# Slot attention with all six products of kept attention and decays on VectorE, and new orders of the four engines' lists

## The reference

```python
q = short_conv(h @ Wq, cq); k = short_conv(h @ Wk, ck)      # 4 taps, silu
v = short_conv(h @ Wv, cv); w = l2norm(short_conv(h @ Ww, cv))
g = log_sigmoid(h @ Wf1 @ Wf2); beta = sigmoid(h @ Wb)
# per head, over the 64 positions of a sequence:
Sk = Sk * exp(g)[None, :] + k[:, None] * (beta * w)[None, :]   # keys by slot
Sv = Sv * exp(g)[:, None] + (beta * w)[:, None] * v[None, :]   # values by slot
a  = softmax(q @ Sk * SCALE)                                   # over the slots
o  = a @ Sv
out = (o * rsqrt(mean(o * o) + eps) * norm_w * sigmoid(gate)) @ Wo
```

## Time and profile before

| | us |
|---|---|
| median of 3 runs | 6353.45 |
| the profiled execution | 6398.69 |
| its span | 6396.9 |
| slot attention in it | from about 80 to 4050 |
| one head of it (four pairs) | 246.8 |
| mean granted TensorE clock of the span | 0.964 |

### The profile page before, as it was taken

The page is one execution under the profiler, slowest core; times in us unless marked ns, Lnnn a source line. Parts: engine busy times, 40 slices in busy tenths (PEclk is TensorE's granted clock), DMA queues, the critical chain, the costliest instruction groups (busy, mean ns, idle before and its releaser), DMA issues. The chain is left out here.

```text
span 6396.9 us, 126892 instructions
## 1 busy us (share of the span) xinstructions
PE 5836.3 (91%) x45072; PEld 4550.3 (71%) x45072; DVE 4333.3 (68%) x8987; ACT 3753.7 (59%) x8473; POOL 1931.1 (30%) x2390
## 2 busy tenths in 40 slices
PE   8999999999999999999999999786889989988879
PEld 5777777777777777777777777675665666667546
DVE  5777777777777777777777777566762237766513
ACT  5677766767766776766777666453651434444313
POOL 2333333333333333333333333232113310001233
PEclk9999999999999999999999999887999999999989
DMA  6200000000000000000000000000002255010124
GB/s 209 65 2 6 5 2 6 4 3 6 1 6 7 1 6 6 2 6 6 2 6 5 2 6 1 28 15 28 2 2 78 91 162 172 2 32 15 60 72 154
DMA packets 164245, 205.77 MB, mean 32 GB/s; under 512 B 22891, under 2 KB 149612, under 8 KB 162928
## 3 DMA queue, kind: packets, MB, share of 16 engines
q1 hardware_dynamic: 148592, 159.99, 8.1%
q0 software_dynamic: 12960, 34.63, 1.5%
q10 hardware_dynamic: 2016, 2.37, 0.1%
HBM read 158.14 MB, written 114.16 MB: 43 GB/s over the span
## 5 line engine op out<-in xcount | busy, mean ns | idle before, releaser
L1713 POOL TENSOR_TENSOR gsa_amb<-gsa_aab,gsa_yb 128x256 f32<-128x256 f32 x64 | 59.9, 937 | 867.7 <-ACT gsa_aab L1565 867.7
L1735 POOL TENSOR_TENSOR gsa_ama<-gsa_aaa,gsa_ya 128x256 f32<-128x256 f32 x64 | 62.4, 975 | 803.0 <-ACT gsa_aaa L1634 803.0
L1548 ACT ACTIVATE gsa_gwva<-PSA,gsa_wcv 128x1024 f32<-128x1024 f32 x64 | 71.2, 1113 | 374.9 <-PE PSA L967 374.9
L1624 ACT ACTIVATE gsa_gwvb<-PSA,gsa_wcv 128x1024 f32<-128x1024 f32 x64 | 71.2, 1113 | 295.8 <-PE PSA L1123 295.8
L955 PE MATMUL PSA<-XT,gsa_wa 128*128 128x512 f32 x256 | 150.0, 716 | 46.7 <-issue 38.5
L1719 POOL TENSOR_TENSOR gsa_ssa<-gsa_ssa,gsa_neghalf 128x4 f32<-128x4 f32 x64 | 64.7, 1011 | 304.3 <-DVE gsa_ssa L1350 304.3
L455 ACT ACTIVATE ffn0b_sl<-PSA 128x512 f32<-128x512 f32 x48 | 28.7, 597 | 207.0 <-PE PSA L162 207.0
L1740 POOL TENSOR_TENSOR gsa_ssb<-gsa_ssb,gsa_neghalf 128x4 f32<-128x4 f32 x64 | 64.4, 1007 | 269.2 <-DVE gsa_ssb L1475 269.2
L263 DVE TENSOR_TENSOR ffn0b_hidden<-ffn0b_sl,PSA 128x512 f32<-128x512 f32 x48 | 33.0, 687 | 163.8 <-ACT ffn0b_sl L455 163.8
L2181 POOL TENSOR_TENSOR mlstm_rs<-mlstm_wide,mlstm_neghalf 128x16 f32<-128x16 f32 x32 | 95.3, 2980 | 140.9 <-DVE mlstm_wide L2058 140.9
L1928 PE MATMUL PSA<-mlstm_XC,mlstm_WIF 128*128 128x128 f32 x512 | 95.5, 363 | 45.7 <-ACT mlstm_XC L2093 45.7
(11 more groups left out here) (758 smaller groups left out, 20366.6 us busy)
## 6 DMA issues: line engine op xcount, KB each, us to landing
pairs<-in_blank SPq DMA_DIRECT2D x2, 35904.0 KB, 126.4
ffn0b_XS<-pairs SPq DMA_DIRECT2D x71, 132.0 KB
ffn1b_XS<-pairs SPq DMA_DIRECT2D x71, 132.0 KB
gsa_wa<-in_w_heads SPq DMA_DIRECT2D x16, 512.0 KB, 3.6
X<-in_x SPq DMA_DIRECT2D x8, 512.0 KB, 6.8
mlstm_CX<-in_ctx SPq DMA_DIRECT2D x32, 128.0 KB, 2.1
ffn0b_WGU<-results SPq DMA_DIRECT2D x8, 512.0 KB, 5.3
ffn0b_WD<-results SPq DMA_DIRECT2D x8, 512.0 KB, 6.0
```

## The change

Only lists in `gsa` change; no shape, buffer, or DMA does.

1. The three products of kept attention and decays that GpSimd did (levels 2, 8 and 32, `AM[:, 0]`, `AM[:, 2]`, `AM[:, 4]`) are issued by VectorE. The semaphores `reach_a_by_pool` and `reach_b_by_pool` go; `reach_a_by_dve` counts six.
2. VectorE's list, from the end of the first three convolution steps on: products 0 and odd, a convolution, product 1, the remaining convolutions (the three of the queries now follow each other), product 4, the identity's, product 2, the first masked copy, decay 0, the norm's sum, product 3, masked copy 2, decay 1, masked copies 3, 4, 5 and 6, decays 2 and 3. Decay 4 goes ahead of the first level addition, and the level step of blocks of 8 ahead of the residual addition.
3. TensorE's list: the two first projections trade places around the last slots product; the two gate products trade places; the transposes of the values and the product of keys and queries stand right behind the transposes of the slot keys; the transposes of decay 1 go ahead of the readout; the first slots product goes ahead of the sum of squares. The waits on GpSimd's masks are for the sixth and the seventh at the first two decayed slots products.
4. ScalarE's list: the two sigmoids trade places; the silu of keys and queries goes ahead of the squares and the first decay's copy; the scaled product of keys and queries ahead of decay 2's copy; the readout's square and the copy of decay 4 behind decay 3's.
5. GpSimd's list: without the three products; the masks in the order odd, diagonal, 3, 2, 4, 0, 1.

The core of the diff, for the half in which slice b is projected and slice a finished (the other half has the same edits):

```diff
 # TensorE
+                        pe.wait_ge(reach_a_by_dve, n * 6 + 3)
+                            last = nc.tensor.matmul(PS[1][:, j * 64:(j + 1) * 64], tile(Ya[:, 1, 512:1024], j), AMa[:, 1, ...
-                        pe.wait_ge(reach_a_by_pool, n * 3 + 2)
                             last = nc.tensor.matmul(PS[0][:, j * 64:(j + 1) * 64], tile(Ya[:, 0, 512:1024], j), AMa[:, 0, ...
                         pe.wait_ge(silu_b_by_act, n * 2 + 1)
                             last = nc.tensor.transpose(tile(PS[4], j), tile(GWVb[:, 512:1024], j), IDENT[:, :])
+                        pe.wait_ge(conv_b_by_dve, n * 9 + 6)
+                            last = nc.tensor.transpose(tile(PS[7], j), tile(GWVb[:, 1024:1536], j), IDENT[:, :])
+                        pe.wait_ge(silu_b_by_act, n * 2 + 2)
+                            last = nc.tensor.matmul(tile(PS[6], j), tile(QKb[:, 512:1024], j), tile(QKb[:, 0:512], j), ...
+                        pe.wait_ge(reach_a_by_dve, n * 6 + 5)
                         pe.wait_ge(weights_a_by_dve, n * 7 + 2)
                             last = nc.tensor.matmul(PS[2][:, j * 64:(j + 1) * 64], tile(Ya[:, 2, 512:1024], j), AMa[:, 2, ...
...
                             last = nc.tensor.transpose(tile(PS[4], j), tile(Yb[:, 1, 512:1024], j), IDENT[:, :])
+                        pe.wait_ge(weights_a_by_dve, n * 7 + 7)
+                            last = nc.tensor.matmul(tile(PS[1], j), tile(GWVa[:, 1024:1536], j), tile(QKa[:, 512:1024], j), ...
...
-                        pe.wait_ge(masked_b_by_pool, n * 7 + 4)
+                        pe.wait_ge(masked_b_by_pool, n * 7 + 6)
                             last = nc.tensor.matmul(PS[6][:, j * 64:(j + 1) * 64], tile(LTb[:, 1, :], j), AMb[:, 0, ...
+                        pe.wait_ge(masked_b_by_pool, n * 7 + 7)
 # VectorE
+                        nc.vector.tensor_tensor(blocks(AMa[:, 0, :], 2), righttiles(AAa[:, :, 0:128], 2), rightblocks(Ya[:, 0, 0:512], 2), ALU.mult).then_inc(reach_a_by_dve, 1)
...
+                        nc.vector.tensor_tensor(blocks(AMa[:, 4, :], 32), ...
+                        nc.vector.tensor_tensor(blocks(AMa[:, 2, :], 8), ...
                         nc.vector.copy_predicated(halves_odd(QKa[:, 512:1024]), ...
+                        nc.vector.tensor_tensor(spread(Yb[:, 0, :], 1), ...
+                        nc.vector.tensor_scalar(ssb[:, :], ssb[:, :], 1e-6, None, ALU.add).then_inc(wnorm_b_by_dve, 1)
+                        nc.vector.tensor_tensor(blocks(AMa[:, 3, :], 16), ...
                         nc.vector.copy_predicated(right(QKa[:, 512:1024], 2), ...
+                        nc.vector.tensor_tensor(spread(Yb[:, 1, :], 2), ...
                         nc.vector.copy_predicated(right(QKa[:, 512:1024], 4), ...
                         nc.vector.copy_predicated(right(QKa[:, 512:1024], 8), ...
-                        nc.vector.tensor_tensor(spread(Yb[:, 1, :], 2), ...
                         nc.vector.copy_predicated(right(QKa[:, 512:1024], 16), ...
+                        nc.vector.tensor_scalar(den2a[:, :], den2a[:, :], 1e-5, None, ALU.mult).then_inc(onorm_a_by_dve, 1)
                         nc.vector.copy_predicated(right(QKa[:, 512:1024], 32), ...
 # GpSimd
-                        nc.gpsimd.tensor_tensor(blocks(AMa[:, 2, :], 8), ...
-                        nc.gpsimd.tensor_tensor(blocks(AMa[:, 0, :], 2), ...
-                        nc.gpsimd.tensor_tensor(blocks(AMa[:, 4, :], 32), ...
```

More of the change, by code:

```diff
@@ L1004, in pair @@
                         last.then_inc(weights_b_by_pe, 1)
-                        pe.wait_ge(reach_b_by_pool, m * 3 + 2)
+                        pe.wait_ge(reach_b_by_dve, m * 6 + 3)
+                        for j in range(4):
+                            last = nc.tensor.matmul(PS[5][:, j * 64:(j + 1) * 64], tile(Yb[:, 1, 512:1024], j), AMb[:, 1, j * 64:(j + 1) * 64], start=True, stop=True)
+                        last.then_inc(weights_b_by_pe, 1)
                         for j in range(4):
@@ L1018, in pair @@
                         last.then_inc(turned_a_by_pe, 1)
+                        pe.wait_ge(conv_a_by_dve, n * 9 + 6)
+                        for j in range(4):
+                            last = nc.tensor.transpose(tile(PS[3], j), tile(GWVa[:, 1024:1536], j), IDENT[:, :])
+                        last.then_inc(turned_a_by_pe, 1)
+                        pe.wait_ge(silu_a_by_act, n * 2 + 2)
+                        for j in range(4):
+                            last = nc.tensor.matmul(tile(PS[2], j), tile(QKa[:, 512:1024], j), tile(QKa[:, 0:512], j), start=True, stop=True)
+                        last.then_inc(keyquery_a_by_pe, 1)
                     if before:
+                        pe.wait_ge(reach_b_by_dve, m * 6 + 5)
                         pe.wait_ge(weights_b_by_dve, m * 7 + 2)
@@ L1063, in pair @@
                         last.then_inc(turned_a_by_pe, 1)
-                    if before:
-                        pe.wait_ge(onorm_b_by_act, m * 1 + 1)
-                        for j in range(4):
-                            last = nc.tensor.matmul(PS[4][:, j:j + 1], tile(QKb[:, 0:512], j), ones[:, 0:1], start=True, stop=True)
-                        last.then_inc(read_b_by_pe, 1)
-                    if within:
                         pe.wait_ge(masked_a_by_pool, n * 7 + 2)
@@ L1075, in pair @@
                     if before:
+                        pe.wait_ge(onorm_b_by_act, m * 1 + 1)
+                        for j in range(4):
+                            last = nc.tensor.matmul(PS[4][:, j:j + 1], tile(QKb[:, 0:512], j), ones[:, 0:1], start=True, stop=True)
+                        last.then_inc(read_b_by_pe, 1)
                         pe.wait_ge(onorm_b_by_dve, m * 3 + 2)
@@ L1147, in pair @@
                         last.then_inc(weights_a_by_pe, 1)
-                        pe.wait_ge(reach_a_by_pool, n * 3 + 2)
+                        pe.wait_ge(reach_a_by_dve, n * 6 + 3)
+                        for j in range(4):
+                            last = nc.tensor.matmul(PS[1][:, j * 64:(j + 1) * 64], tile(Ya[:, 1, 512:1024], j), AMa[:, 1, j * 64:(j + 1) * 64], start=True, stop=True)
+                        last.then_inc(weights_a_by_pe, 1)
                         for j in range(4):
@@ L1151, in pair @@
                         last.then_inc(weights_a_by_pe, 1)
-                        pe.wait_ge(reach_a_by_dve, n * 3 + 3)
-                        for j in range(4):
-                            last = nc.tensor.matmul(PS[1][:, j * 64:(j + 1) * 64], tile(Ya[:, 1, 512:1024], j), AMa[:, 1, j * 64:(j + 1) * 64], start=True, stop=True)
-                        last.then_inc(weights_a_by_pe, 1)
-                        pe.wait_ge(sigmoid_b_by_act, n * 2 + 1)
+                        pe.wait_ge(sigmoid_b_by_act, n * 2 + 2)
                         pe.wait_ge(silu_b_by_act, n * 2 + 1)
@@ L1195, in pair @@
                         last.then_inc(turned_b_by_pe, 1)
+                        pe.wait_ge(weights_a_by_dve, n * 7 + 7)
+                        for j in range(4):
+                            last = nc.tensor.matmul(tile(PS[1], j), tile(GWVa[:, 1024:1536], j), tile(QKa[:, 512:1024], j), start=True, stop=True)
+                        last.then_inc(read_a_by_pe, 1)
                         pe.wait_ge(decay_b_by_act, n * 5 + 3)
@@ L1201, in pair @@
                         last.then_inc(turned_b_by_pe, 1)
-                        pe.wait_ge(onorm_a_by_act, n * 1 + 1)
-                        for j in range(4):
-                            last = nc.tensor.matmul(PS[0][:, j:j + 1], tile(QKa[:, 0:512], j), ones[:, 0:1], start=True, stop=True)
-                        last.then_inc(read_a_by_pe, 1)
                         pe.wait_ge(masked_b_by_pool, n * 7 + 2)
@@ L1210, in pair @@
                         last.then_inc(slots_b_by_pe, 1)
+                        pe.wait_ge(onorm_a_by_act, n * 1 + 1)
+                        for j in range(4):
+                            last = nc.tensor.matmul(PS[0][:, j:j + 1], tile(QKa[:, 0:512], j), ones[:, 0:1], start=True, stop=True)
+                        last.then_inc(read_a_by_pe, 1)
                         if gp == 0:
```

363 lines of the change are left out of this document (156 added, 207 removed).

## The result

The changed kernel takes 6620.65 us (median of 4 runs, 6615.44 to 6623.99), the kernel before 6355.26 (4 runs): ratio 1.0417, 95% interval 1.0399 to 1.0435. The forecast was 6425 us with 6345 to 6492 as its range: right in sign, wrong in size, 265 us instead of 72. The profiled execution took 6623.99 us with a span of 6621.9.

A forecast was written before the change was run, and what follows sets the result against it. It took TensorE's in-order list to bound slot attention, stalling for ScalarE and VectorE. 0.52 + 0.08 = 0.60 us per half, times 128 = 77 us, less 5, scaled to +71.5 on 6353.45: 6425 us, range 6345 to 6492.

The forecast's parts named there:

- ScalarE's stretch up to the keys' transposes: Softmax transpose to slot keys' transposes, 10.78 us set by gapless ScalarE: change 0, ends -0.1 to +0.2 us.
- The rival on this place: ScalarE's stretch gets shorter through the sigmoids' exchange: at most 0.2 us per half, 6330 us; chance 0.10.
- The prediction's own sign of being wrong: Softmax transpose to slot keys' transposes: a move of more than 0.1 us would show the forecast wrong.
- The readout: Slot keys' transposes to readout: VectorE's last masked copy comes later, so the readout starts 0.52 us late per half.
- 1.03 of VectorE's 1.40 us: VectorE's list before the last masked copy: 1.40 us longer, 1.03 of it for the three products from GpSimd.
- Behind the readout: Readout to first decayed slots product: +0.08 us, 0.05 for VectorE and GpSimd taking turns, 0.03 for the next step.
- The cover of 0.4 us: Behind the readout: ScalarE's scaled keys and queries end about 1108.1, TensorE needs them at 1108.51, covered by 0.4.
- The rival on SBUF's shared side: GpSimd's masks giving way to VectorE delay the seventh mask, square and slots copy: 0.5 us per half, 6489 us; chance 0.14.
- From the product to the next softmax transpose: First decayed slots product (L1220) to the next half's softmax transpose (L972): change 0.
- The sum: Whole half: 0.52 + 0.08 = 0.60 us, times 128 halves = 77 us.

The follow-up runs named there:

- e1: Changed kernel with the two gate products and the two sigmoids back in the old order; 1.0255 of the kernel before.
- e2: Kernel before with one unused semaphore increment on ScalarE between the wait for the first gate product and the first sigmoid; 1.0521.
- e8: Changed kernel with gate products and sigmoids in the old order and GpSimd's seven masks cut to one column (masking left out); 1.0091 of the kernel before.
- e4: Changed kernel with the denominators' factor moved back ahead of masked copy 2; 1.0396 of the kernel before.
- e10: e8 with VectorE's three added products (decays 0, 2 and 4) also cut to four columns; 1.0074 of the kernel before.
- e5: Changed kernel with GpSimd's seven masks cut to one column each (masking left out); 1.0305 of the kernel before.
- e3: Kernel before with only the three products moved from GpSimd to VectorE, all other lists as before; 1.0415.
- e6: e2 with the kept product ahead of the slot keys' transposes computed twice, filling TensorE's stall; 1.0128 of the kernel before.
- e9: Changed kernel with e1's and e4's edits and decay product 2 between masked copies 4 and 5; 1.0175 of the kernel before.

## Why the prediction was wrong

**ScalarE's stretch up to the keys' transposes: the step that failed.** The prediction took 0 (-0.1 to +0.2) since "the number and kind of its steps is the same". The kind of the wait in front of the first sigmoid was not: it became a wait of its own, the table's load moved behind it, +0.76 us per half. e1 takes it away, e2 makes it. The rival on this place had only the other sign. The row of the load was not among the rows read; it would have shown that 0.65 us of it lay ahead of the gate product's end. The prediction's own sign of being wrong, this stretch moving by more than 0.1 us, came true.

**The readout: +0.52 forecast, +0.74 found.** With the other two costs gone it is 0.50 (e8). The 0.24 above that are the denominators' factor, 0.69 us beside GpSimd's mask instead of 0.15, whose move to that place the working did not count (e4: 0.23). But the size came near for a reason that does not hold in the changed kernel, so the agreement is in good part luck. The working put 1.03 of VectorE's 1.40 us down to the three products. These stand ahead of L1448, where VectorE is idle for 0.58 us; what sets the copies there is the wait for ScalarE's squares, which the change moved ahead of five copies and which the working passed over. Only with the keys' transposes back in their place (e1, e8) does VectorE's list decide, and even there 0.43 of the 0.50 stay with the products taken away (e10).

**Behind the readout: +0.08 forecast, +0.49 found.** The mechanism was named, decay product 2 beside the diagonal mask, and the rows for it were there. Its first reader had no term. The cover of 0.4 us was worked out for the scaled keys and queries; TensorE's transposes of decay 2 come before these in its list, due 0.99 us behind the readout's start, and the product is done 1.34 us after that start. The prediction's own times, a product of 0.68 us begun at about 1108.0 and a readout at 1107.08, would have made it 0.6 us late. The rival on SBUF's shared side gave 0.5 us per half, at the seventh mask, the square and the slots copy; the price came out and the place did not. The Trainium skill ("GPSIMD Engine Reference", section "8. Key points") names two kinds of VectorE instructions that contend with GpSimd: those in a 2-port perf mode and those with two SBUF inputs. The decay products, with two, agree (1.50 us beside a mask, 0.68 in e5). L1469 has one tensor input of four elements a partition, and GpSimd's masks made it four times as long (0.69, against 0.16 in e5). It could only be of the first kind, and no trace here shows the mode of an instruction. For the forecast it is enough that a small step lengthens too.

**From the product to the next softmax transpose: 0 forecast, 0 found** (8.68 us in every run).

**The clock.** The prediction had no step for it. In the changed kernel it is 0.1 to 0.2%; in e2 and e3, which put one part of this change each into the kernel before, it is most of the loss by the time at the half clock, and e6 shows it for e2.

**The sum.** Forecast 0.60 us per half, found 1.98, of which 0.76 + 0.74 + 0.49 as above. With the 2.11 of the other kind of half, 64 pairs make 262 of the 265 us. The few us between this and the 268 that slot attention grew by are not split up: clock falls are in the means and not in these medians, and the loops' turns differ a little (2.73 us of issue idle for L951 in the changed kernel, 3.05 before).

Open is what the products alone cost in the new order. It would take the norm's small step back behind the copies; but GpSimd's factor and ScalarE's scaled products hang on that step, so this would be one more new wait, and it was not tried.

## What to carry to other kernels

When two steps that look alike trade places, compare how each one waits, and look where the activation table's load lies: the part of a load that was hidden in a wait is paid when an instruction stands between the wait and the activation. When a list is reordered, follow each step that lands beside GpSimd's work, the small ones too, to whoever waits for it next. When a step is moved ahead of others, look at what it waits for: everything behind it inherits the wait. A stall of TensorE of about a microsecond may cost more by the clock than by itself (e2), and one cheap probe, the last product once more in the stall, tells how much.

## What was not expected of the hardware

- A table load runs ahead of a wait that its activation carries (started at 1096.23, with the awaited product done near 1096.9), but not ahead of a wait that stands apart (0.77 us idle first, 0.80 in e2).
- TensorE's granted clock: with a stall of 0.44 us per half 89 us of slot attention are at 1.2 GHz, with 1.20 us 645, with the same stall filled 113. The changed kernel has the same 1.20 us stall and only 197: what follows the stall there is the same work in another order. What makes this difference was not found.
- A VectorE step on 128 x 4 elements took 0.69 us beside a GpSimd mask, and 0.15 to 0.17 where it lay elsewhere (the kernel before, e3, e4, e9) or where the masks were cut to one column (e5, e8, e10).
